# Writing out the batch loops of a one-core adaLN block on all five engines

## The reference

```
mod = (silu(c) @ wmod) -> sa, ca, ga, sb, cb, gb          (8 x 1024 each)
ga, gb = sign * max(|.|, 0.25)
attn = (w1^T w2^T) * sparse_mask                          (1024 x 1024)
h = layernorm(x) * (1 + ca) + sa
x = x + ga * gelu(h @ attn + b2)
h = layernorm(x) * (1 + cb) + sb
P = h @ U1 (rank 256);  H = P @ V1 + b1;  act = silu(gate) * up   (2752 wide)
x = x + gb * (act @ U2 @ V2 + b2)
```

## Time and profile before

| | before |
|---|---|
| median of 3 runs (lowest, highest) | 1271.64 us (1271.54, 1274.2) |
| span of the profiled execution | 1272.8 us |
| PE matmul busy | 1200.2 us, 94% |
| DVE, ACT, POOL busy | 54%, 30%, 19% |
| instructions | 15879 |

### The profile page before, as it was taken

One profiled execution on the slowest core, in us unless ns is written; L12 is line 12 of the kernel. 1 busy time (PEld: TensorE's weight loads), 2 busy tenths in 40 slices (PEclk: granted clock), 3 DMA queues, 4 the chain that ended last, 5 costly groups with the idle time before them and its releaser, 6 DMA issues.

```text
span 1272.8 us, 15879 instructions
## 1 busy us (share of the span) xinstructions
PE 1200.2 (94%) x5617; PEld 956.4 (75%) x5617; DVE 683.4 (54%) x1104; ACT 388.0 (30%) x645; POOL 239.6 (19%) x194
## 2 busy tenths in 40 slices
PE   7877999999999899999999989999999999999995
PEld 4445678877777688788878868878877887887884
DVE  0838699999996433453363353363353336336335
ACT  0122334444433454223322312223322331332230
POOL 0023322233222364120030030030011003003003
PEclk9899899999999899999999989999998999999998
DMA  9796644544447453050050031013004004003001
GB/s 347 280 382 242 238 166 182 214 181 181 192 181 272 169 169 124 28 176 1 1 182 1 1 119 64 1 57 126 1 24 160 1 1 162 20 1 115 35 1 66
DMA packets 51168, 154.71 MB, mean 122 GB/s; under 512 B 4640, under 2 KB 8992, under 8 KB 49056
## 3 DMA queue, kind: packets, MB, share of 16 engines
q1 hardware_dynamic: 51104, 153.79, 33.2%
HBM read 111.80 MB, written 41.98 MB: 121 GB/s over the span
## 4 chain that ended last, share of the span: by engine, by line
issue 56%; PE 24%; DVE 8%; POOL 8%; DMA 2%; ACT 1%; SPq 1%; POOLq 0%; DVEq 0%; ACTq 0%
POOL x2t L1360 6%; PE bank L469 5%; PE bank L471 5%; PE bank L470 5%; PE bank L539 4%; DVE nrm L1024 2%; PE bank L635 2%; DMA x<-in_x 2%; PE bank L504 1%; DVE bn L1182 1%; DVE h_lo L1125 1%; DVE bn L1014 1%; DMA wm_sb<-in_wmod 1%; POOL g L1308 1%; DVE xr L1177 1%
## 5 line engine op out<-in xcount | busy, mean ns | idle before, releaser
L1236 DVE SCALAR_TENSOR_TENSOR act<-bank,b_sb,act 128x512 f32<-128x512 f32 (+1 forms) x176 | 131.9, 750 | 411.9 <-PE bank L471 394.0
L961 ACT ACTIVATE act<-bank,b_sb 128x512 f32<-128x512 f32 (+1 forms) x176 | 121.3, 690 | 546.9 <-PE bank L471 529.3
L469 PE MATMUL bank<-pt,v_hi 128*128 128x512 f32 x688 | 270.9, 394 | 7.7 <-issue 6.2
L470 PE MATMUL bank<-pt,v_hi 128*128 128x512 f32 x688 | 269.7, 392 | 0.0
L471 PE MATMUL bank<-pt,v_lo 128*128 128x512 f32 x688 | 269.6, 392 | 0.0
L1360 POOL TENSOR_TENSOR x2t<-ffn,x2t 128x512 f32<-128x512 f32 x64 | 89.9, 1410 | 677.0 <-DVE ffn L1272 677.0
L469 PEld LDWEIGHTS bank<-pt,v_hi 128*128 128x128 f32 x688 | 130.2, 189 | 38.4 <-issue 9.6
L471 PEld LDWEIGHTS bank<-pt,v_lo 128*128 128x128 f32 x688 | 130.3, 189 | 27.3
L470 PEld LDWEIGHTS bank<-pt,v_hi 128*128 128x128 f32 x688 | 130.3, 189 | 26.8
L469 PE MATMUL bank<-act_hi,u_hi 128*128 128x512 f32 (+1 forms) x352 | 138.3, 393 | 0.9 <-DVE act_lo L1243 0.9
L471 PE MATMUL bank<-act_hi,u_lo 128*128 128x512 f32 (+1 forms) x352 | 137.0, 389 | 0.0
(11 more groups left out here) (111 smaller groups left out, 1519.5 us busy)
## 6 DMA issues: line engine op xcount, KB each, us to landing
wm_sb<-in_wmod SPq DMA_DIRECT2D x10, 2048.0 KB, 12.4
xr<-in_x SPq DMA_DIRECT2D x16, 1024.0 KB, 6.9
x_dram<-xr SPq DMA_DIRECT2D x16, 1024.0 KB, 4.4
x2t<-x_dram SPq DMA_DIRECT2D x32, 512.0 KB, 3.9
out<-x2t SPq DMA_DIRECT2D x32, 512.0 KB, 4.6
xs<-in_x SPq DMA_DIRECT2D x7, 2048.0 KB, 8.1
pt_dram<-pt_st SPq DMA_DIRECT2D x8, 1024.0 KB, 3.9
pt<-pt_dram SPq DMA_DIRECT2D x8, 1024.0 KB, 5.8
```

Source lines behind the costliest of these rows:

```text
L469: nc.tensor.matmul(acc, s_hi, m_hi, start=start, stop=False)
L470: nc.tensor.matmul(acc, s_hi, m_lo, start=False, stop=False)
L961: nc.scalar.activation(act[0:w, i % 2, :], bank[0:w, i % 2, :], ACT.Silu, bias=b1_sb[0:w, i, 0:1]).then_inc(silu_done, 1)
L1236: nc.vector.scalar_tensor_tensor(act[0:w, i % 2, :], up, b1_sb[0:w, i, 1:2], act[0:w, i % 2, :], ALU.add, ALU.mult).then_inc(act_done, 1)
```

## The change

In ten places, two on each engine, a hardware loop becomes a Python `range`, so that the same calls are emitted once per batch with constant batch numbers; the order within each engine is unchanged, and no branch goes back.

```diff
-            with sp.Fori(1, NB - 2) as b:
+            for b in range(1, NB - 2):
                 iteration(b, True, True, True)
...
-            with pe.Fori(2, NB - 1) as b:
+            for b in range(2, NB - 1):
                 iteration(b, True, True, True)
...
-            with pe.Fori(1, NB // 2) as i:
+            for i in range(1, NB // 2):
                 batch(i * 2 - 1, 1, False)
                 batch(i * 2, 0, False)
...
-            with pool.Fori(1, NB - 1) as b:
+            for b in range(1, NB - 1):
                 iteration(b, True)
...
-            with pool.Fori(0, NB) as b:
+            for b in range(0, NB):
                 residual(b)
```

More of the change, by code:

```diff
@@ L457, in _ @@
             batch(0, 0, False)
-            with sp.Fori(1, NB // 2) as i:
+            for i in range(1, NB // 2):
                 batch(i * 2 - 1, 1, False)
@@ L949, in _ @@
             iteration(1, True, True, True)
-            with ae.Fori(2, NB - 1) as b:
+            for b in range(2, NB - 1):
                 iteration(b, True, True, True)
@@ L988, in _ @@
             batch(0, 0, False)
-            with ae.Fori(1, NB // 2) as i:
+            for i in range(1, NB // 2):
                 batch(i * 2 - 1, 1, False)
@@ L1217, in _ @@
             iteration(1, True, True, True)
-            with dve.Fori(2, NB - 1) as b:
+            for b in range(2, NB - 1):
                 iteration(b, True, True, True)
@@ L1282, in _ @@
             batch(0, 0, False)
-            with dve.Fori(1, NB // 2) as i:
+            for i in range(1, NB // 2):
                 batch(i * 2 - 1, 1, False)
```

## The result

| | before | after |
|---|---|---|
| median (runs) | 1272.92 us (4) | 1263.13 us (4) |
| lowest, highest | 1271.54, 1274.69 | 1262.83, 1263.83 |
| span of the profiled execution | 1272.8 | 1262.0 |
| instructions | 15879 | 14465 |

The ratio is 0.9927, 95% interval 0.9914 to 0.9940: 9.8 us faster between the medians where 12.5 were forecast, and 0.6 us above the upper end of the range. The device time of the profiled execution after is 1263.83 us, 1.8 us more than its span; every run on record has 1.7 to 1.9 us between the two. So the profile before, with a span of 1272.8, is of a run of some 1274.6 us, the slowest of its four.

A forecast was written before the change was run, and what follows sets the result against it. PE, busy 94% of the span, was taken as the bound, with two taken stage-two branches costing stalls and slow clock. 12.12 + 0.4 = 12.5 us off 1271.64 gave 1259.1 us, range 1256.5 to 1262.5.

The forecast's parts named there:

- PE's stage-two branches (-12.12): PE's two taken branches at line 820: removing them saves 12.12 us, 6.2 of stalls and 5.9 of slow clock.
- A (the clock falls anyway): Stage two: the 1.2 GHz limit comes without the stop, so only the stalls go; 1265.0 us, chance 5%.
- C (a boundary in the stream): Stage two: straight code stalls at the same spot, time stays at about 1271.2 us; chance 3%.
- More instructions to fetch ... I take 0: Stage one, streamed four times more by PE: bounds 0 and 0.55 us, taken as 0; 1.3 us kept for skips.
- rival B: Stage one's written-out forward skips at line 616 stall for fetches, losing 22 us; 1281 us, chance 3%.
- The stall that the prediction expects of PE's stage-one branch by the Trainium skill: By a two-line, 16 KiB each, rule, four taken branches would stall: 4 x 6 us more gain, near 1235 us.
- PE's stage-one branch (0): Four taken branches of 0.21 us each, covered by PE's 0.96 us wait for DVE's norm; value 0.
- Register operations (-0.4): Stage one: PE starts 0.08 us sooner after DVE's norm in each of five iterations, saving 0.4 us.
- POOL's residual (0): Starts a few hundredths earlier, changing its overlap with DVE's line 1272; ends -6.9 and +5.4 us, taken as 0.
- rival D: POOL and DVE overlap better, winning 0.4 us more in each of eight batches; 1255.9 us, chance 6%.
- The base: The median of the kernel before, 1271.64 us, from which the forecast subtracted its 12.5 us.

The follow-up runs named there:

- e1: Kernel before with only PE's stage-two loop written out, all other loops kept; 1259.96 us, ratio 0.9917.
- e2: Kernel before with only PE's stage-one loop written out, all other loops kept; 1275.87 us, ratio 1.0030.
- e3: Changed kernel with PE's stage-one loop kept, all other loops written out; 1259.77 us, ratio 0.9914 to the kernel before.
- e5: Changed kernel with 96 never-executed instructions added in the skipped block at line 490, shifting PE's later stream; 1261.21 us, ratio 0.9911 to the kernel before.
- e6: Changed kernel with 256 never-executed instructions, one 16 KB fetch, added in the skipped block at line 490; 1262.62 us, ratio 0.9922 to the kernel before.
- e10: Changed kernel with PE's stream shifted by 96 never-executed instructions and both POOL loops kept; 1260.71 us, ratio 0.9904 to the kernel before.
- e4: Changed kernel with POOL's stage-two loop kept, all other loops written out; 1264.24 us, ratio 0.9948 to the kernel before.
- e9: Kernel before with batches 1 and 2 of PE's stage two written out, leaving one taken branch of two; 1266.15 us, ratio 0.9950.
- e8: Kernel before, all loops kept, skipped blocks at line 616 six times as long, PE's stage-one body 1987 instructions; 1340.13 us, ratio 1.0545.
- e11: The changed kernel run again, all ten loops written out, against the kernel before; 1263.25 us, ratio 0.9927.

## Why the prediction was wrong

- **What bounds, and PE's stage-two branches (-12.12): right.** The seven windows of stage two take 12.11 us less in e1's profile, and both halves of the price, the stall and the slow clock, are gone. Rivals A (the clock falls anyway) and C (a boundary in the stream) are wrong with it.
- **"More instructions to fetch ... I take 0": the step that failed.** I asked only whether PE would stall for its own stream, and it did not: the skips at line 616 stayed at most 0.333 us, as before, so rival B is wrong too. I did not ask what a fetch does to the transfers beside it. It delayed one store by 1.9 us, with 0.6 us of slack: 1.4 us more of idle PE, and the slow clock after it the other 1.6. Measured +2.95 where I had 0 and kept at most 1.3 us, for skips. e2 and e3 show that it comes and goes with PE's stage-one loop, e5 and e6 that it comes and goes with the place of the fetch. That the last packets of the store ran one at a time, and only once the fetch was over, fits a fetch and a sixteenth of the store on one of the 16 DMA engines; the views do not name the engine. Without these 2.95 us the time would have been 1260.2, inside the range.
- **The stall that the prediction expects of PE's stage-one branch by the Trainium skill: a misreading.** The section cited (Runtime: NRT & Kernel Launch, Instruction fetch mechanics) gives the two lines for a memory of 32 KiB, and gives PE one of 128 KiB, 2048 instructions. The trace agrees with neither as the limit of a loop on PE: 727 and 1231 instructions go round without a stall, 1846 do not.
- **PE's stage-one branch (0): right.** The four windows from batch 2's to batch 6's first turn_back take 155.05 us before and 155.14 after.
- **Register operations (-0.4): wrong in size, 0.** PE does start 0.055 us after the norm in place of 0.14, as forecast. But DVE's four norm instructions take 4.75 us together, before 4.67: they begin at 219.75 and end at 224.50. With only PE's loop written out (e2) they already take 4.72 to 4.74, with all but PE's (e3) 4.69 to 4.70, and e10 clears POOL's registers. That PE's earlier `y` makes POOL's work overlap the norms more is argued, not shown.
- **POOL's residual (0): mis-sized, +0.6.** 0.09 us in each of seven windows, shown by e4 and e10. It is inside the bounds kept, on the losing side, so rival D (a better overlap) is wrong.
- **The 0.15 of one window** comes with the constants of DVE, ACT or SP (e3, e4 and e10 have it, e1 and e9 not). A DVE instruction of line 1236 starts 0.35 us late there, after 2.51 us of idle time in place of 2.16; why is open.
- **The base.** The median of three runs was 1271.64; over 49 runs of the kernel before in four groups the medians are 1271.7 to 1272.9, with runs from 1267.65 to 1275.33. A base of 1272.92 would have put the forecast 1.3 us higher and the upper end of the range at 1263.8, so the measured time lies outside the range by the base and the late store together. Against 1272.92, the sum -12.1 + 2.95 + 0.6 + 0.15 gives 1264.5; measured 1263.13. The 1.4 us between are not accounted for.

## What to carry to other kernels

A loop whose body outgrows what the engine can hold of its stream pays at every taken branch, and on PE then again in the clock. Here writing out that loop alone gave as much as any kernel measured, while PE's loop that fitted cost nothing and kept fetches away from the data transfers. When a change adds instruction fetches, look for the transfers on the critical path with less than 2 us of slack (this store had 0.6 and came 1.9 late), in the iterations that were written out before too. Where a fixed loss of some us appears far from the edit, shift the stream by less than one piece and by exactly one: what goes with the first and comes back with the second is a matter of alignment.

## What the runs showed of the hardware

- A stall of 3.1 us on PE cost 6.1: the granted clock was 0.50 for some 5.5 us after it. One of 3.6 us (e9) cost 5.5, with 3.4 us at 0.50. After the idle stretch of 2.25 us in stage one it was 0.50 for 3.4 us as well.
- A fetch of 16 KB beside a store of 1 MB made it land in 4.17 to 5.78 us in place of 3.85 to 4.22.
- The same idle stretch can go either way. Every kernel waits 2.0 us for `z_lo` in the last batch; in e10 the clock fell during it, in the changed kernel's first profile it did not, and the time from the last `out_product` to the end was 24.3 against 22.0 us. It is not the kernel alone that decides: e11, the changed kernel again, took 24.5. The five kernels that keep PE's stage-two loop, whole or in part, took 23.3 to 23.4, with a fall just after the wait; the nine profiles without it never did. e10's rows:

```profile
1229.50:1234.40 4.90, 3.23 (x12) 2.08 (x12) 1.63 (x3) 1.64 (x3) 0.00 (x0) 1.00 0.01 3
1234.40:1241.20 6.80, 5.90 (x14) 4.66 (x15) 1.91 (x4) 0.01 (x1) 0.00 (x0) 0.50 0.00 0
```

- The prologue, which waits for loads, took from 107.3 to 111.4 us up to the first turn_back over the profiles of all kernels but e8. I take these two for most of the spread between runs of one kernel; it was not tested.
